# Requesting all four groups of expert weights in one block at the first shared tile of each expert stage

## The reference

```
shared = silu_and_mul(x @ shared_gate_up_w.T) @ shared_down_w.T      # hidden 704
shared = shared * sigmoid(x @ sgate_w.T)
routing_weights = softmax(x @ gate_w.T)                              # 16 experts
topk_w, topk_ids = top_k(routing_weights, 4)
for e in experts:
    coef = sum(where(topk_ids == e, topk_w, 0))
    acc += (silu_and_mul(x @ w13[e].T) @ w2[e].T) * coef             # hidden 176
out = shared + acc
```

## Time and profile before

| | |
|---|---|
| median of three executions | 1252.41 us (1249.12 to 1254.31) |
| profiled execution, its own time | 1253.93 us |
| its span | 1252.0 us |
| mean granted clock of TensorE | 0.967 |
| busy: PE, DVE, ACT, POOL | 94%, 64%, 60%, 48% |
| chain that ended last | PE 80%, DVE 6%, DMA 6%, issue 4% |
| expert stage 0: first request of weights to first expert tile | 355.37 to 424.21 us |
| expert stage 1: the same | 1043.56 to 1118.81 us |
| requests of groups 1, 2, 3 in stage 0 | 371.61, 411.73, 415.99 us |
| requests of groups 1, 2, 3 in stage 1 | 1060.05, 1102.25, 1110.47 us |

### The profile page before, as it was taken

The page is one execution under the profiler, slowest core; times in us unless marked ns, Lnnn a source line. Parts: engine busy times, 40 slices in busy tenths (PEclk is TensorE's granted clock), DMA queues, the critical chain, the costliest instruction groups (busy, mean ns, idle before and its releaser), DMA issues.

```text
span 1252.0 us, 23038 instructions
## 1 busy us (share of the span) xinstructions
PE 1175.0 (94%) x7484; PEld 1008.6 (81%) x7484; DVE 807.0 (64%) x2038; ACT 752.3 (60%) x1734; POOL 600.4 (48%) x497
## 2 busy tenths in 40 slices
PE   6999999999897899989999999999999989489997
PEld 5878888888784777768999999999999988377775
DVE  7766767777882433477777777777777787143335
ACT  5866667666551333427888887887888865033332
POOL 3211222121137165625776777677776643705663
PEclk9999999999997899989999999999999998789999
DMA  3366766653245777741322222232222015556665
GB/s 114 88 181 169 175 174 174 170 162 71 58 153 203 181 137 137 129 103 51 89 77 59 59 61 65 61 70 79 59 75 59 17 48 158 201 168 112 117 116 145
DMA packets 94277, 141.59 MB, mean 113 GB/s; under 512 B 8184, under 2 KB 73976, under 8 KB 93048
## 3 DMA queue, kind: packets, MB, share of 16 engines
q1 hardware_dynamic: 74400, 102.32, 29.8%
q0 software_dynamic: 15744, 20.98, 9.8%
q10 hardware_dynamic: 4056, 17.30, 4.6%
HBM read 99.71 MB, written 40.86 MB: 112 GB/s over the span
## 4 chain that ended last, share of the span: by engine, by line
PE 80%; DVE 6%; DMA 6%; issue 4%; ACT 2%; POOL 1%; SPq 0%; DVEq 0%; ACTq 0%; POOLq 0%
PE ps L276 20%; PE ps L278 19%; PE ps L277 19%; PE ps L1116 7%; PE ps L1141 5%; DMA sums_d<-e_y,xg 3%; PE ps L551 2%; DMA rows_a<-a_rows_d 1%; PE ps L1129 1%; PE ps L1093 1%; DVE valT L762 1%; PE ps L1680 1%; PE ps L565 1%; DMA a_vg_raw<-a_vg 1%; DVE x L1419 1%
## 5 line engine op out<-in xcount | busy, mean ns | idle before, releaser
L1291 POOL DMA_INDIRECT sums_d<-e_y,xg x88 | 137.6, 1564 | 137.2 <-ACT e_y L1218 79.8
L1116 PE MATMUL ps<-w,e_xT 128*128 (+1 forms) x376 | 127.2, 461 | 2.5 <-ACT e_xT L1201 1.7
L1412 DVE COPY e_hT<-ps 88x256 f32<-88x256 f32 x94 | 39.5, 420 | 132.0 <-PE ps L1129 118.0
L427 POOL TENSOR_TENSOR aw_lo<-aw_raw,aw_hi 128x512 fp32r<-128x512 f32 x32 | 42.0, 1317 | 152.5 <-ACT aw_hi L423 152.5
L276 PE MATMUL ps<-xn_hi,aw_hi 128*128 128x512 f32 x256 | 111.2, 434 | 2.7 <-DVE bmat_lo L790 2.7
L857 DVE TENSOR_TENSOR m_a<-ps,e_a 128x384 f32<-128x384 f32 x128 | 71.3, 557 | 58.5 <-PE ps L551 57.9
L278 PE MATMUL ps<-xn_hi,aw_lo 128*128 128x512 f32 x256 | 101.4, 396 | 0.0
L277 PE MATMUL ps<-xn_lo,aw_hi 128*128 128x512 f32 x256 | 100.9, 394 | 0.0
L1141 PE MATMUL ps<-w,e_hT 88*128 (+1 forms) x376 | 96.7, 379 | 0.0
L656 ACT COPY late<-ps 128x256 f32<-128x256 f32 x128 | 47.7, 373 | 69.7 <-PE ps L278 69.6
L427 POOL TENSOR_TENSOR ms_b_lo<-m_b,ms_b_hi 128x384 fp32r<-128x384 f32 x64 | 65.0, 1017 | 49.2 <-ACT ms_b_hi L423 49.2
(11 more groups left out here) (311 smaller groups left out, 4145.8 us busy)
## 6 DMA issues: line engine op xcount, KB each, us to landing
rows_a<-a_rows_d SPq DMA_DIRECT2D x64, 256.0 KB, 5.1
xg<-slots_d SPq DMA_DIRECT2D x94, 144.0 KB
slots_d<-slot_init SPq DMA_DIRECT2D x10, 1152.0 KB, 6.9
w<-moe_up ACTq DMA_DIRECT2D x8, 1408.0 KB
wconv_raw<-b_conv SPq DMA_DIRECT2D x16, 513.0 KB
aw_raw<-a_heads SPq DMA_DIRECT2D x32, 256.0 KB, 3.0
wvo_raw<-b_vo SPq DMA_DIRECT2D x16, 512.0 KB, 3.4
rows_b<-b_rows_d SPq DMA_DIRECT2D x32, 256.0 KB, 4.8
```

Of the source, the lines that this page charges most:

```text
L427: return nc.gpsimd.tensor_tensor(dst[1], src, f32(dst[0]), ALU.subtract).then_inc(sem(done_sem), 1)
L1116: ins = nc.tensor.matmul(ps[:, 2 + t % 2, 0:2 * E_HIDDEN], e_xT[:, t % 2, k], weights_of(w13, t, at_w, k * 2 * E_HIDDEN, 2 * E_HIDDEN), st ...
L1291: nc.gpsimd.indirect_dma_start(sums_d[f][t % CHAINS], bass.IndirectOffsetOnAxis(ap=xg[:, t % XG, ROW_ID:ROW_ID + 1].bitcast(U32), axis=0), ...
L1412: nc.vector.tensor_copy(e_hT[0:HALF_E, t % 2], ps[0:HALF_E, 4 + t % 2, 0:2 * P].rearrange("p (j m) -> p j m", j=2)).then_inc(sem("e_hT"), 1)
```

## The change

The table is gone, and the loop over shared tiles no longer asks for weights. Groups 1, 2 and 3 are asked for one behind the other, before the loop, in both expert stages. Lines behind the change stand two lower.

```diff
-        W_AFTER = {1: 1, 3: 2, 4: 3}
-
         def f_w_act(act, g):
...
             f_hi_act(act, f, 0, 1)
             f_up_weights_act(act, f, 2)
             f_down_weights_act(act, f, 1)
+            for g in range(1, W_GROUPS):
+                f_w_act(act, g)
             for i in range(1, S_TILES):
                 for c in range(CHUNKS):
                     f_silu_act(act, f, i, c)
...
                 if i + 2 < S_TILES:
                     f_up_weights_act(act, f, i + 2)
-                if i in W_AFTER:
-                    f_w_act(act, W_AFTER[i])
```

## The result

| | before | changed kernel |
|---|---|---|
| median of 21 executions each | 1253.41 us | 1256.54 us |
| ratio | | 1.0034 (1.0018 to 1.0050) |
| profiled execution, its span | 1252.0 us | 1251.4 us |

The changed kernel is 3.1 us slower; the forecast was 4.3 us faster. The two profiled spans must not be subtracted: the executions of one kernel spread over some 10 us, and this one of the changed kernel was its second fastest. What the two traces do tell is where each expert stage lost or won against its own start. As marks I take the first `f_s` of a stage and the turn of expert tile 3 (its `e_xT`), the first tile that needs all four rounds of scatters.

What follows compares the result with a forecast made beforehand. It took two holes of some 24 us, where PE is slow beside POOL's scatters, to bound the kernel. Terms -8.9 + 1.9 + 2.7 = -4.3 us gave 1248 us against a median of 1252.41; range 1236 to 1266.

Steps and rivals of the forecast that it cites:

- If PE keeps the 0.35 us pace while weights flow: Both expert stages: longer weight flow beside scatters lifts PE from 1.10 to 0.35 us per matmul, 8.9 us gained.
- three pace readings beside traffic and three without separate cleanly: Argument that PE's pace depends on weight traffic: about 0.35 us per matmul beside it, 1.10 beside scatters alone.
- Tile 3's delay: SP's load of shared tile 3, now beside the weights, comes 4.0 us later; PE idles that much in the first stage.
- Fits inside the lag: nothing: Second stage: PE's effects lag until 1070.92 us, so shared tile 3's later load costs nothing there.
- Its price in the stretch: First stage: PE idling 4.0 us leaves 11.4 matmuls undone when the hole ends, costing 1.9 us afterwards.
- the first rival: PE's pace has nothing to do with the weights; only shared tile 3's delay is left: 1254.3 us, chance 0.22.
- The earlier start of the middle pace: Weights and scatters meet about 8 us earlier per stage; PE may slow sooner, nothing to 8.2 us lost, 2.7 taken.
- The second rival: Weights queued ahead of scatters start PE's slowest pace 8 us earlier per stage: 1267.8 us, chance 0.28.
- ACT's own time: Six weight requests of 0.42 us delay tile 1's first f_s by 2.5 us; cost 0.1 us, taken as nothing.
- Groups 2 and 3: Their absence beside the last shared tiles saves nothing, as PE is gapless there even at a 0.97 DMA share.
- The third rival: PE stays at 0.17 us while weights flow, only the last scatters bind: half the gain gives 1234 us, chance 0.12.
- The signs looked for: Requests in one block, weights until about 400 and 1088, last scatter at 407; wrong if PE's gaps start before 380.

Runs made afterwards that it cites:

- e17: Weight groups 1 to 3 asked for after shared tiles 3, 4, 5, against the kernel before, with PE's slow stretch beside the scatters: ratio 1.0004.
- e18: Weight groups 1 to 3 in one block behind shared tile 1, against the kernel before, with PE's slow stretch: ratio 1.0002.
- e6: The changed kernel, unchanged, against the kernel before, in a group without PE's slow stretch: 1225.31 us against 1216.08, ratio 1.0077.
- e13: The changed kernel, unchanged, against the kernel before, in a group with PE's slow stretch: 1257.41 us against 1251.85, ratio 1.0043.
- e14: The changed kernel with shared tile 3 loaded first to memory of its own, against the kernel before, with PE's slow stretch: ratio 0.9984.
- e15: Weight groups 1 and 2 at the first shared tile, group 3 behind tile 1, against the kernel before, with PE's slow stretch: ratio 1.0045.
- e2: Weight groups 1 to 3 after shared tiles 3, 4, 5, against the kernel before, without PE's slow stretch: 1228.82 us, ratio 1.0113.
- e11: Repeat of e2, weight groups after shared tiles 3, 4, 5, against the kernel before, without PE's slow stretch: ratio 1.0109.
- e9: Weight groups 1 and 2 asked for behind shared tile 1, group 3 behind tile 2, against the kernel before, without PE's slow stretch: ratio 1.0005.
- e10: The order of e9, with shared tile 3 loaded first to memory of its own, against the kernel before, without PE's slow stretch: ratio 1.0012.
- e4: Only weight group 1 moved to the first shared tile, against the kernel before, without PE's slow stretch: ratio 1.0068, 7.4 us slower.

## Why the prediction was wrong

**The step that failed** is "If PE keeps the 0.35 us pace while weights flow", -8.9 us. The runs show nought in its place. The times were read rightly, but their order in time was taken for a cause: in the kernel before, the end of group 1 and the fall merely came together. e17 removes the weights and keeps the fall; e18 and the changed kernel itself have weights flowing beside 0.7 to 1.3 us per matmul. The argument "three pace readings beside traffic and three without separate cleanly" counted readings that all lay in one order in time, fast first and slow later, so the time since the scatters began separated them just as well. Nor was 0.35 us one pace: it was read once from 12 up matmuls and once from 24 down matmuls. At the full pace of 0.23 and 0.12 us each, shown below, both take some 2.8 us; 4.30 us is 1.5 times that, 8.26 us 2.9 times, and the slow readings are 4.8 to 8.5 times. The prediction called this a coincidence that decides, and gave the theory without it 0.22.

**Tile 3's delay** was the right mechanism at half its size: 4.0 us forecast, 8.3 us measured in the first profile (10.0 us from the start of its stage), 9.3 to 9.4 us of waiting on PE in e6 and e13. I had taken the delay of tile 4's load beside one group. That load was asked for in the same half microsecond as the group; tile 3's now comes 8 us behind the first of six requests, and it moved no packet for 5 us. (The "five routing operations" on that path are six, lines 1483 to 1488.) "Fits inside the lag: nothing" held for the second stage in the first profile, which even gained 0.9 us.

**Its price in the stretch**, 4.0 us for 1.9, scales to 3.9 us for 8.3, or 4.8 for 10.0; the first stage lost 3.8. With the forecast's two other terms gone, the first rival with the right delay gives 1252.4 + 3.9 = 1256.3 us, a ratio of 1.0031; measured were 1256.54 us and 1.0034. With 10.0 us it would be 1257.2 us and 1.0038, inside the interval as well. The close match is luck in part: no run tests this price, and the repeat in e13, held against the profile of the first kernel before, has 4.5 and 0.3 us for the two stages, and 1.0043. That rival, "PE's pace has nothing to do with the weights", was the true case and only its number was off.

**The earlier start of the middle pace**, +2.7, did not come. In the changed kernel PE went through tile 1's and half of tile 2's work at 0.12 and 0.23 us per matmul beside a share of 1.04, until it ran dry at 376.18. These are times of issue; that the work was also done on pace shows in e14. The second rival falls with it: there PE is on pace until 384.06 in the first stage, with three groups queued and scatters since 365 us, and in the second until 23.0 us after its first `f_s`, where the kernel before has 20.5.

**ACT's own time** was forecast at 2.5 us, of which 0.1 us would show, "taken as nothing". It took 5.3 us in the first stage (360.42 to 365.74) because the third request hung. PE waited only 0.6 us for it directly (0.2 in e6), but the forecast had overlooked the path from tile 1's `f_h` over DVE to SP's request for tile 3: on it the requests cost 1.7 us in the first profile, 1.3 in e6 and nothing in e15. This small term is contained in the 10.0 us of delay.

**Groups 2 and 3** beside the last tiles: right with the stretch. Without it their place matters, since they compete with the scatters and gathers that the expert tiles wait for (e2, e11).

**The third rival**, a large gain, was half seen from the wrong side: without the stretch the last scatters do bind the first expert tiles, but in the kernel before already.

**The signs looked for.** The requests did stand in one block, the weights did flow until 396 us, the last scatter stayed at its place. But two of the signs of being wrong came: PE's gap started before 380 us, and ACT's third `moe_up` took far longer than 0.42 us. "PE's matmuls get sparse only after that" was wrong on the first count: 31 instead of 65 from 372 to 384. The stretch after 388 holds 47 for 14, but these are issued and not done: ACT got only twelve of the 48 matmuls before 396 us. In the second stage there are 43 instead of 11 from 1073 to 1085, and 8 instead of 5 after that.

## What to carry to other kernels

A bulk load that nobody needs soon must not be asked for ahead of a small load on another queue that the next step needs. Look for every request that is issued during the bulk's flow, not only for those beside it now, and count the time before its first packet as well as its share afterwards. Times of two traces are compared from the start of their own stage: here a request that seemed to have kept its place was 1.7 us late.

When a slow phase and a fast phase are compared, look for a kernel or a stage in which the suspected cause and the order in time come apart, before the difference is priced. And a delay on the critical engine is worth its full length only where no later wait, here for scatters and gathers, is longer; find that wait first.

## What the runs showed of the hardware

- PE's completions can fall from 0.12 to 0.23 us to about 1 us per matmul (0.65 to 1.0 for 24 down matmuls, 0.7 to 1.35 for 12 up matmuls) beside POOL's indirect scatters, with issue gaps that no wait explains. The last semaphore that came on pace was 8 us (1062.66 against 1054.49, kernel before, second stage) to 26 us (390.53 against 364.62, changed kernel) after the first scatter, and the pace was back some 4 to 5 us after the last was issued. It showed in some groups of runs and in others not at all, for the same kernels, and was worth 36 us here. POOL issues a scatter every 1.3 us in both (32 within 42 us).
- Three groups of requests queued on one DMA queue held the requesting sequencer for 2.6 to 4.7 us in the fifth request; with two groups queued each took 0.33 to 0.8 us (e9, e10, e15).
- A load on SP's queue, asked for while ACT's queue held over 4 MB, moved nothing for 5 us and landed after 11.8 us (11.7 in e13, 11.9 in e15); behind one group it took 9.1 us (e4), alone 3.5 us.
